# Moving one depthwise tap from ScalarE and GpSimd to VectorE, and one copy from GpSimd to ScalarE

## The reference

```
pooled = x.mean((2, 3));  hdn = layernorm(pooled @ w_fc1.T)
dyn_w  = (hdn @ w_fc2.T)                        # a 5x5 kernel for each image and channel
out = depthwise_conv5x5(x, dyn_w)               # own taps for each image and channel
out = channel_layernorm(out) * ln2_w + ln2_b
out = gelu(einsum('bchw,oc->bohw', out, w_expand))      # 64 -> 256 channels
gx  = sqrt(sum(out**2, (H, W)));  nx = gx / mean(gx)
out = gamma * (out * nx) + beta + out
return einsum('bohw,co->bchw', out, w_shrink) + x       # 256 -> 64 channels
```

## Time and profile before

| | us |
|---|---|
| median of 3 runs | 850.76 (849.52 to 851.38) |
| the profiled execution | 850.89 |
| span of its trace, first to last instruction | 849.2 |
| of the span, `block_two` | 502 to 849 |
| TensorE busy | 782.8 |
| VectorE busy | 616.4 |
| GpSimd busy | 468.0 |
| ScalarE busy | 408.8 |

### The profile page before, as it was taken

How to read it: one execution, slowest core, us unless ns; L and a number is a source line. 1 busy time by engine, 2 the same in 40 slices (tenths; PEclk the granted TensorE clock), 3 DMA queues, 4 the chain that set the end, 5 groups by cost and what they waited for, 6 DMA issues and landing times. The chain is left out here.

```text
span 849.2 us, 15642 instructions
## 1 busy us (share of the span) xinstructions
PE 782.8 (92%) x5399; PEld 637.7 (75%) x5399; DVE 616.4 (73%) x1130; ACT 408.8 (48%) x497; POOL 468.0 (55%) x458
## 2 busy tenths in 40 slices
PE   5999999999999999999999968587899999999796
PEld 5999998999999999999999966354444545444231
DVE  4666666666666666658888866988799898998944
ACT  5591003777771000000000014369899999999771
POOL 2333333333333333337888854788889889897510
PEclk9999999999999999999999987889899999999899
DMA  6760000000000000000000010132233443334314
GB/s 146 154 173 0 0 0 2 0 0 0 0 1 1 0 0 0 0 1 2 0 0 0 0 49 0 47 77 58 52 79 81 112 97 94 78 80 91 83 32 100
DMA packets 61572, 35.81 MB, mean 42 GB/s; under 512 B 41504, under 2 KB 59488, under 8 KB 61536
## 3 DMA queue, kind: packets, MB, share of 16 engines
q1 hardware_dynamic: 61536, 35.36, 18.0%
HBM read 17.85 MB, written 9.37 MB: 32 GB/s over the span
## 5 line engine op out<-in xcount | busy, mean ns | idle before, releaser
L481 PE MATMUL psum<-line_hi,taps_hi 128*128 128x256 f32 x1270 | 202.5, 291 | 11.8 <-DVE taps_lo L377 8.5
L495 PE MATMUL psum<-line_lo,taps_hi 128*128 128x256 f32 x1270 | 202.2, 291 | 0.8 <-DVE line_lo L430 0.8
L489 PE MATMUL psum<-line_hi,taps_lo 128*128 128x256 f32 x1270 | 202.0, 291 | 0.0
L430 DVE SCALAR_TENSOR_TENSOR line_lo<-psum,rest 128x256 fp32r<-128x256 f32 x254 | 108.2, 426 | 123.4 <-POOL rest L262 114.9
L481 PEld LDWEIGHTS psum<-line_hi,taps_hi 128*128 128x128 f32 x1270 | 176.6, 192 | 12.9 <-issue 9.3
L495 PEld LDWEIGHTS psum<-line_lo,taps_hi 128*128 128x128 f32 x1270 | 176.3, 191 | 1.9 <-DVE line_lo L430 1.7
L489 PEld LDWEIGHTS psum<-line_hi,taps_lo 128*128 128x128 f32 x1270 | 176.7, 191 | 0.0
L262 POOL TENSOR_TENSOR rest<-x,line_hi 128x256 f32<-128x256 f32 x127 | 82.8, 652 | 167.8 <-DVE line_hi L421 167.8
L759 POOL TENSOR_TENSOR part<-part,prod 128x960 f32<-128x960 f32 (+2 forms) x64 | 145.2, 2269 | 25.0 <-ACT prod L826 17.8
L262 POOL TENSOR_TENSOR rest<-by_h,line_hi 128x256 f32<-128x256 f32 x127 | 91.5, 720 | 83.4 <-DVE line_hi L421 83.4
L314 ACT ACTIVATE by_h<-x (+1 forms) x128 | 85.7, 669 | 105.0 <-DVE x L410 103.3
(11 more groups left out here) (138 smaller groups left out, 749.5 us busy)
## 6 DMA issues: line engine op xcount, KB each, us to landing
stage<-in_x_dram SPq DMA_DIRECT2D x32, 256.0 KB, 4.1
rstd_wide<-rstd_dram SPq DMA_DIRECT2D x30, 256.0 KB, 5.4
out_dram<-x SPq DMA_DIRECT2D x28, 256.0 KB, 5.5
crossed<-x SPq DMA_DIRECT2D x16, 256.0 KB, 3.6
crossed<-x SPq DMA_DIRECT2D x16, 240.0 KB, 3.5
out_dram<-x SPq DMA_DIRECT2D x8, 128.0 KB, 2.5
rstd_dram<-rstd SPq DMA_DIRECT2D x15, 64.0 KB, 1.5
fc_in<-in_L_conv_w_fc_dram SPq DMA_DIRECT2D x2, 100.0 KB
```

Of the source, the lines that this page charges most:

```text
L430: dve.scalar_tensor_tensor(out=line_lo[:, (slot + 1) % SLOTS, :, part], in0=as_lines(line_ps[slot][:, 0:LINE]), scalar=0.0, in1=as_lines(r ...
L481: mm = pe.matmul(line_ps[slot][:, 0:LINE], taps_hi[:, s, d, :], line_hi[:, slot, :, d:d + WP], start=(d == 0), stop=(d == OFFSETS - 1))
L489: pe.matmul(line_ps[slot][:, 0:LINE], taps_lo[:, s, d, :], line_hi[:, slot, :, d:d + WP], start=False, stop=False, skip_group_check=True)
L495: mm = pe.matmul(line_ps[slot][:, 0:LINE], taps_hi[:, s, d, :], line_lo[:, slot, :, d:d + WP], start=False, stop=(d == OFFSETS - 1), skip_ ...
```

## The change

The tap ("up", 3) goes from the products of ScalarE to the taps of VectorE. `DVE_TAPS` grows from ten to eleven; the new one is the tenth, and is so taken in `take(N_DVE)` at the end of the slot, after `respond`. `ACT_TAPS` shrinks from five to four, and with it `N_ACT` and the number of GpSimd's sums, from four to three a unit. The copy x to `x_hi` for units 2 to 15 goes from GpSimd's queue to ScalarE's, where it is issued behind the first gelu of slot s for unit s + 2, with a wait for the convolution of unit s. ScalarE's products between the gelus are regrouped, so that there are still two instructions behind the first gelu (the copy and a product) and two behind the third. Units 0 and 1 had their copy on ScalarE already.

```diff
@@ constants @@
 DVE_TAPS = [("cross", 0), ("cross", 1), ("cross", 3), ("cross", 4), ("up", 0), ("up", 4), ("down", 0), ("down", 4),
-            ("down", 3), ("cross", 2)]
+            ("down", 3), ("up", 3), ("cross", 2)]
 MIDDLE = [("down", 2), ("up", 2)]
-SIDES = [("up", 1), ("down", 1), ("up", 3)]
+SIDES = [("up", 1), ("down", 1)]
@@ GpSimd @@
-            def split_high(u):
-                pool.wait_ge(conv_done, 2 * (u - 1))
-                pool.tensor_copy(x_hi[:, u % 2, :, 2:2 + W],
-                                 x[:, u // 2, ROWS * (u % 2):ROWS * (u % 2 + 1), :]).then_inc(xhi_ready, 1)
-
@@
                 if s + 2 < UNITS:
-                    split_high(s + 2)
                     split_low(s + 2)
@@ ScalarE @@
             def split_high(u):
+                if u >= 2:
+                    act.wait_ge(conv_done, 2 * (u - 1))
                 act.activation(x_hi[:, u % 2, :, 2:2 + W], x[:, u // 2, ROWS * (u % 2):ROWS * (u % 2 + 1), :],
                                ACT.Copy).then_inc(xhi_ready, 1)
@@
-                for i, between in enumerate(((1, 2), (), (3, 4), ())):
+                for i, between in enumerate(((1,), (), (2, 3), ())):
                     if e in range(UNITS):
                         gelu(e, i // 2, i % 2)
                     if i == 1 and e in range(UNITS):
                         add_squares(e, 0)
+                    if i == 0 and s >= 0 and s + 2 < UNITS:
+                        split_high(s + 2)
```

## The result

The changed kernel took 860.15 us (median of 4 runs, 857.64 to 861.18) against 851.07 us (4 runs, 849.52 to 853.47) for the kernel before. The ratio is 1.010, with a 95% interval of 1.0067 to 1.0132. The forecast was 859.8 us. The execution with the profile is the fastest of the four, 857.64 us with a span of 855.9 us, so its trace has 6.7 us more than the one of before and not 9.1.

The account below looks back on a forecast made before the run. VectorE bounds even slots from L1008 to the root, ScalarE and TensorE odd ones. Start 2.8 us plus steady slots 6.3 us makes 9.1 us, giving 859.8 us; own range 858.0 to 861.5, wider range 853.5 to 863.5.

Parts of the forecast that it names:

- The even slots: Behind `respond`, from L1008 to the root, VectorE is the chain: the tap costs 1.23 us in each of five slots.
- TensorE's wait for `inner`: In even slots from 6 on, TensorE's convolution now waits for `inner`, some 0.8 us.
- the root's wait: In even slots, ScalarE's root waits for VectorE's variance from 0.40 to about 0.8 us.
- The wait in front of L1008: Even slots: VectorE's 1.65 us wait hangs on the same slot's root, can't absorb the tap, falls to about 1.0 us.
- its cover: Odd slots: VectorE's 1.3 us spare hides the 1.30 us tap; 0.03 us a slot put on it.
- Slot 4: Tap behind this slot's `respond` is hidden: VectorE has 0.62 us in hand and ScalarE's table load covers the same again.
- The start: Units 0 and 1: VectorE is the chain, so taps of 0.75, 0.77 and 1.30 us cost 2.8 us before ScalarE's gelus.
- The end: Last unit: its `inner` comes 2.5 us later, still ahead of ScalarE's square; nothing is added.
- the forecast's 6.3: Steady slots: five even slots at 1.23 us and five odd ones at 0.03 us make 6.3 us.
- Hidden taps: Rival: even slots' tap is swallowed by the 1.65 us wait, only the start costs, 853.6 us; chance 0.10.
- GpSimd gives time back: Rival: GpSimd's 6.6 us less work a pair speeds VectorE up, 850 to 851 us; chance 0.05.
- TensorE's clock: Rival: its fall at 600 to 618 goes, 857.0 us, chance 0.10; or more falls, 862.6 to 865.4 us, chance 0.13.

Follow-up runs that it names:

- e4: Changed kernel with two taps instead of one taken between the second finish and `respond`; 852.81 us, ratio 1.0019.
- e7: Changed kernel with the eleventh tap cut to one column in even units from 2 on; 854.44 us, ratio 1.0042.
- e6: Changed kernel with the eleventh tap cut to one column in odd units from 3 on; 861.56 us, ratio 1.0127.
- e10: Kernel before with added matmuls, whose result nobody reads, in TensorE's idle stretches; 846.50 us, ratio 0.9939.
- e8: Changed kernel with the eleventh tap cut to one column in units 0 and 1 alone; 857.96 us, ratio 1.0076.
- e11: Changed kernel with added matmuls, whose result nobody reads, in TensorE's idle stretches; 857.21 us, ratio 1.0061.
- e5: Kernel before, same ten taps, with two instead of one taken between the second finish and `respond`; 850.28 us, ratio 0.9991.
- e12: Kernel before with two taps in front of `respond` and added unread matmuls in TensorE's idle stretches; 844.64 us, ratio 0.9905.
- e1: Changed kernel with the copy to `x_hi` left on GpSimd, so only the tap moves; 859.41 us, ratio 1.0085.
- e3: Changed kernel with the eleventh tap cut to one column in every unit; 852.15 us, ratio 1.0022.

## Why the prediction was right, and where it wasn't

**The even slots** held in every step. The tap took 1.22 us of the chain (1.23 forecast), L1008 to root 13.64 us (13.6), the pair 37.22 us (37.25). TensorE's wait for `inner` came out at 0.88 us (0.8) and its wait for the gelu at 1.01 us (1.0), the root's wait at 0.78 us (0.8). e4 and e7 show the mechanism: take the tap out of the stretch behind L1008, or cut it there, and the loss in the pair is gone but for the 0.28 us of the cut one; e6 shows that the odd slots have no part in it.

**The wait in front of L1008** did hang on the root of its own slot: root to L1006 is 715.77 - 709.90 = 5.87 us, 5.88 before. It was forecast to fall to 1.0 us and fell to 1.36. The reason is the odd slot: its cover was a little larger than worked out. VectorE's variance there ended at 746.24 + 0.32 + 0.29 = 746.85 and the root came at 747.12, 0.27 us later, where I had the cover used up. The tap's own 1.30 us was right (four taps in 738.05 - 733.05 = 5.00 us, three in 3.69). The two idle times of the earlier trace rows miss two bits of cover, which show from start to start. VectorE in the odd slot, before and then with the change:

```profile
734.64 2.56 DVE L958 SCALAR_TENSOR_TENSOR psum<-crossed,tap_cross,psum 128x992 f32<-128x992 f32 x2
737.30 0.75 DVE L1028 SCALAR_TENSOR_TENSOR x<-psum,out_bias,x 128x512 f32<-128x512 f32 x1
...
740.43 0.15 DVE L1003 TENSOR_REDUCE resp<-energy 128x2 f32<-128x4 f32 x1
```

```profile
740.58 2.56 DVE L956 SCALAR_TENSOR_TENSOR psum<-crossed,tap_cross,psum 128x992 f32<-128x992 f32 x2
743.04 0.75 DVE L1026 SCALAR_TENSOR_TENSOR x<-psum,out_bias,x 128x512 f32<-128x512 f32 x1
...
746.17 0.15 DVE L1001 TENSOR_REDUCE resp<-energy 128x2 f32<-128x4 f32 x1
```

`finish` came 2.66 us after the start of the taps in front of it and now comes 2.46 us after it: 0.20 us, too short a wait to be listed. And before L975 it was 741.23 - 740.43 = 0.80 us, now 746.24 - 746.17 = 0.07: 0.73 us of cover, where the listed idle time is 0.66. Together that is the 0.27 us.

**Slot 4** is the term that was left out. I took its tap as hidden because VectorE had 0.62 us in hand behind it in the trace of before. It had that only because TensorE's clock had fallen just there. That held VectorE up for 3.24 us at L1008 (2.17 in e10, at a clock of 1.00), but it held ScalarE up by more: two of its gelus stood for an expand. VectorE and the two gelus in slot 4 of the kernel before, then VectorE in slot 4 of the changed kernel, and ScalarE's root behind it:

```profile
603.03 0.16 DVE L1008 TENSOR_SCALAR resp<-psum 128x1 f32<-128x1 f32 x1 [3.24 <-PE psum L1228]
```

```profile
605.04 1.11 ACT L855 ACTIVATE wide<-psum,expand_bias 128x1024 f32<-128x1024 f32 x1 [0.99 <-PE psum L1219]
...
609.70 1.11 ACT L855 ACTIVATE wide<-psum,expand_bias 128x1024 f32<-128x1024 f32 x1 [1.54 <-PE psum L1219]
```

```profile
604.13 0.16 DVE L1006 TENSOR_SCALAR resp<-psum 128x1 f32<-128x1 f32 x1 [2.16 <-PE psum L1226]
```

```profile
617.77 0.40 ACT L839 ACTIVATE std<-var,eps_col 128x128 f32<-128x128 f32 x1 [0.76 <-DVE var L975]
```

In the changed kernel's trace the fall came a slot earlier (0.91 in 581 to 599, 1.00 in 600 to 618), the root behind slot 4 waited 0.76 us for VectorE, and its interval (617.77 - 598.26) was 19.51 us like the others; the fall cost slot 3 0.9 us (598.26 - 579.76 = 18.50 us, 17.60 before). e8, which is the changed kernel in slot 4, shows the other case: there the clock fell in slot 4, as before, and the slot took 20.70 us with the whole tap, the same as the 20.70 us (616.78 - 596.08) of the kernel before without it. e10 without the tap and without the fall took 18.27 us. So there are six slots that pay, not five, when the clock is up there.

**The start** is 2.8 us by the forecast, and 2.81 us of VectorE's time in e11 against e10. In the changed kernel's own trace the first gelu came only 0.24 us later (563.85 - 512.69 against 562.54 - 511.62 us, from `tap_all`). The clock gave the rest back in that execution: from the first matmul at the heads of slots 1 and 2 to ScalarE's L837 (L833 of the changed kernel) behind the sums it took 5.29 and 5.30 us instead of 6.24 and 6.43, and from unit 0's first matmul to VectorE's first tap 5.26 instead of 5.76, 2.6 us together. The other three runs had a mean clock of 0.967 to 0.968 instead of 0.974, so they were at the lower level for longer, and took 860.0 to 861.2 us.

**The end** did not add nothing; two terms cancelled, and the forecast had neither. Slot 15, from its root to the last one, took 822.32 - 803.85 = 18.47 us, before 813.85 - 796.77 = 17.08. TensorE had stood 3.66 us there, before 0.49, and its clock in the slot was 0.63, before 0.85. Behind the last `respond` it went the other way, at a clock of 1.00 instead of 0.88. TensorE in the changed kernel, then before:

```profile
806.73 2.08 PE L1217 MATMUL psum<-normed,expand_w 64*128 64x512 f32 x4 [3.66 <-ACT wide L851]
...
844.34 7.09 PE L1241 MATMUL psum<-wide,shrink_now 128*64 128x512 f32 x32 [1.24 <-DVE shrink_now L1017]
```

```profile
835.87 8.78 PE L1243 MATMUL psum<-wide,shrink_now 128*64 128x512 f32 x32 [1.24 <-DVE shrink_now L1019]
```

The last 32 matmuls took 7.09 instead of 8.78 us. e11 and e10 have the same two terms: slot 15 is 1.2 us longer (18.48 against 17.28 us), and the stretch from the last L1008 on 1.2 us shorter (14.5 against 15.7 us, at 0.88 and 0.73). No run tested whether the second follows from the first.

**Accounts of the trace.** First block +1.1 us, start +0.2, slots 2 to 5 (first gelu to slot 6's root) -0.3, slots 6 to 14 +6.1, end -0.4, together 6.7 us. The 6.1 us are the forecast's 6.3. Why the first block, the same code in both, took 1.1 us more in this trace is open; in the traces of e5 and e12, built from the kernel before, it took 0.8 and 0.5 us more as well, and over all traces it lies between 0.1 us less (e10) and 1.5 us more (e1), so it does not go with the change.

**The rivals.** Hidden taps: fell. GpSimd gives time back: fell, by e3. TensorE's clock: neither of its two forms came alone, but in small steps: at the heads of the first slots the number of matmuls at the lower level differs from one execution to the next, and the mean clock of a run goes with its time over the spread from 849 to 854 us. The rival had one fall at 2.8 us as its price; keeping TensorE busy at the heads of slots 1 and 2 and in slots 2 to 4 was worth 5.2 us (851.7 us beside e10, and 846.5). The Trainium skill ("TensorE: Matmul & The Clock Gate", What's actually happening) ties the clock to how busy the array has been; the runs agree, since matmuls without use held it at 1.00 between 600 and 618 us, where it had been 0.81.

That the sum met the median, 859.8 against 860.15, is partly luck. The forecast left out the 1.2 us of slot 4 and 1.2 to 1.4 us in slot 15, and the 1.1 us of the first block; with the clock held up in the filled stretches the change costs 10.7 us. Between the two kernels as they are it is 9.1 us, since each meets its own low clock, which can cover a tap (slot 4 of e8) or shorten the end.

## What to carry to other kernels

Here VectorE had 3 us of idle time in 36, and still no room for 2.5 us of work behind its wait, only in front of it. Before an instruction is added: find the wait, see what it hangs on, and put the new instruction ahead of it. Moving one tap ahead of `respond` turned a loss of 9 us into one of 1 to 2. And before a gain of a few microseconds is sought in the order of the engines, look at whether TensorE's clock falls in idle stretches on the chain; here keeping it busy was worth 5.2 us to the kernel before, and the earlier tap at most 2.

## What was not expected of the hardware

A VectorE instruction on 15 or 16 elements per partition still took 0.28 us of its engine in a row of taps. Ten matmuls of 512 columns behind an idle stretch of 6.12 us ran at the lower clock in full in one execution (0.63 us each) and the first seven of ten in another behind 7.62 us, so the length of the idle stretch alone doesn't say how long the low clock lasts; what does was not tried.
